# A two-branch graph convolution on one core: part of the row sums of tiles 4 to 11 taken from blocks that are loaded anyway

## The reference

```
d    = (sum(adj, axis=1) + 1e-9) ** -0.5
H_f  = relu((d[:,None] * adj * d[None,:] @ x)         @ W_f + b_f)
H_s  = relu((d[:,None] * adj * d[None,:] @ spatial_x) @ W_s + b_s)
attn = sigmoid(concat(H_f, H_s) @ W_att + b_att)
y    = x + attn * H_f + (1 - attn) * H_s
out  = (y - mean(y)) / sqrt(var(y) + 1e-5)          # over a row
```

## Time and profile before

| | |
|---|---|
| median of 3 runs | 420.37 us (420.26 to 420.81) |
| the profiled execution | 420.79 us, of which 419.0 us are its span |
| mean granted clock of PE | 0.971 |
| PE matmuls | 375.0 us busy, 90%, x1680 |
| PE weight loads | 309.4 us busy, 74% |
| DVE | 289.3 us busy, 69% |
| ACT | 286.1 us busy, 68% |
| POOL | 146.3 us busy, 35% |
| DMA | 132.84 MB, mean 317 GB/s |

### The profile page before, as it was taken

The page is one execution under the profiler, slowest core; times in us unless marked ns, Lnnn a source line. Parts: engine busy times, 40 slices in busy tenths (PEclk is TensorE's granted clock), DMA queues, the critical chain, the costliest instruction groups (busy, mean ns, idle before and its releaser), DMA issues. The chain is left out here.

```text
span 419.0 us, 5128 instructions
## 1 busy us (share of the span) xinstructions
PE 375.0 (90%) x1680; PEld 309.4 (74%) x1680; DVE 289.3 (69%) x401; ACT 286.1 (68%) x346; POOL 146.3 (35%) x199
## 2 busy tenths in 40 slices
PE   0689998699969999999899999999999999998940
PEld 0567887588858887888678888888888888887830
DVE  2569983496366957597655959388757886977554
ACT  3768588877888749787888687674433676576453
POOL 1203001021000881059200899251000556643664
PEclk9999999999989999999989999999999999999965
DMA  8999999999999999999999999897555444350001
GB/s 312 389 425 421 417 422 421 421 421 420 422 420 422 415 342 418 422 419 422 423 418 422 413 415 375 320 380 268 199 190 187 192 128 165 111 175 27 25 26 51
DMA packets 25530, 132.84 MB, mean 317 GB/s; under 512 B 2848, under 2 KB 7712, under 8 KB 11296
## 3 DMA queue, kind: packets, MB, share of 16 engines
q1 hardware_dynamic: 25504, 132.53, 79.1%
HBM read 130.42 MB, written 2.10 MB: 316 GB/s over the span
## 5 line engine op out<-in xcount | busy, mean ns | idle before, releaser
L356 PE MATMUL sums<-Ah,Yh 128*128 128x512 f32 x512 | 203.4, 397 | 25.5 <-DVE Yl L432 18.3
L421 DVE TENSOR_TENSOR Al<-raw,Ah 128x2048 fp32r<-128x2048 f32 (+1 forms) x70 | 152.3, 2179 | 90.7 <-ACT Ah L552 89.5
L358 PE MATMUL sums<-Al,Yh 128*128 128x512 f32 x512 | 201.4, 393 | 0.0
L357 PE MATMUL sums<-Ah,Yl 128*128 128x512 f32 x512 | 201.3, 393 | 0.0
L552 ACT ACTIVATE Ah<-raw 128x2048 fp32r<-128x2048 f32 (+1 forms) x70 | 123.4, 1767 | 54.2 <-DMA raw<-in_At 30.2
L356 PEld LDWEIGHTS sums<-Ah,Yh 128*128 128x128 f32 x512 | 97.6, 191 | 49.0 <-DVE Yl L432 19.5
L565 ACT ACTIVATE nat<-nat 128x2048 f32<-128x2048 f32 x53 | 101.6, 1917 | 19.2 <-DMA nat<-in_adj 17.9
L358 PEld LDWEIGHTS sums<-Al,Yh 128*128 128x128 f32 x512 | 97.3, 190 | 20.7
L357 PEld LDWEIGHTS sums<-Ah,Yl 128*128 128x128 f32 x512 | 97.7, 191 | 19.8
L444 DVE TENSOR_TENSOR acc<-sums,acc 128x512 f32<-128x512 f32 x112 | 71.5, 682 | 6.3 <-PE sums L358 6.3
L657 POOL TENSOR_SCALAR dg<-rs 128x1 f32<-128x1 f32 x22 | 14.1, 640 | 150.6 <-ACT nat L565 150.3
(11 more groups left out here) (43 smaller groups left out, 112.1 us busy)
## 6 DMA issues: line engine op xcount, KB each, us to landing
raw<-in_At SPq DMA_DIRECT2D x63, 1024.0 KB, 10.0
nat<-in_adj SPq DMA_DIRECT2D x56, 1024.0 KB, 11.6
xs<-in_xs SPq DMA_DIRECT2D x7, 512.0 KB, 11.2
out<-xs SPq DMA_DIRECT2D x32, 64.0 KB, 1.7
raw<-in_At SPq DMA_DIRECT2D x4, 256.0 KB, 9.8
xs<-in_xs SPq DMA_DIRECT2D x1, 384.0 KB, 9.2
xs<-in_xs SPq DMA_DIRECT2D x1, 128.0 KB, 2.4
watt<-in_W_att SPq DMA_DIRECT2D x1, 128.0 KB, 10.3
```

What stands on the lines that cost most here:

```text
L356: pe.matmul(to, Yh[:, t % YRING, hs], high, start=first, stop=False)
L357: pe.matmul(to, Yl[:, t % YRING, hs], high, start=False, stop=False)
L358: mm = pe.matmul(to, Yh[:, t % YRING, hs], low, start=False, stop=last)
L421: dve.tensor_tensor(Al[:, k % SPLITS, a * IB:b * IB], raw[:, k % RAWS, a * IB:b * IB], Ah[:, k % SPLITS, a * IB:b * IB], ALU.subtract).the ...
```

## The change

1. Groups 1 and 2 (tiles 4 to 11) get the treatment of groups 6 and 7 in small. Their blocks of inner tiles below their own first tile (tiles 0 to 3 for group 1, 0 to 7 for group 2), 12 in items 0, 1, 4, 5 and 8 to 11, are added up by POOL in the planes of `S`; the first block of a plane is copied instead of added, and the clearing of `S` goes. PE sums the planes over partitions after items 6 and 12 (`collect_early`), DVE copies the sums to `early` ahead of the low parts of items 8 and 14 (`early_sums`), and POOL takes them as the third term of the degree. The parts of these tiles shrink to half of the remaining columns: 1792 for tiles 4 to 7, 1536 for tiles 8 to 11 (before, 2048).
2. The load of part 4 moves ahead of item 3; part 5 stays ahead of item 4.
3. Features: groups 1 to 7 are loaded after items 6, 12, 20, 28, 36, 39 and 43 (before: 6, 7, 15, 23, 31, 39, 47). `y_position` keeps the items of the Y of tiles 12 to 31.
4. The evacuation of the run that ends in items 15, 23 and 31 is done ahead of the low parts of items 17, 25 and 33.

```diff
+    EARLY_SUMS = {1: 6, 2: 12}
+    PLANE = {1: 0, 2: 1, G - 2: 0, G - 1: 1}
     parts = {k: [] for k in range(K)}
-    for k, r in [(0, 0), (1, 1), (4, 2), (5, 3), (8, 4), (9, 5), (10, 6), (11, 7)]:
+    for k, r in [(0, 0), (1, 1), (5, 3), (8, 4), (9, 5), (10, 6), (11, 7)]:
         parts[k] = [2 * r, 2 * r + 1]
+    parts[3], parts[4] = [4], [5]
...
-                if OWN_COLUMNS <= k < FINAL and runs[e][0] in BY_COLUMN]
+                if (OWN_COLUMNS <= k < FINAL and runs[e][0] in BY_COLUMN)
+                or (runs[e][0] in EARLY_SUMS and t < runs[e][0] * GT)]
 
     def blocks_summed(k):
         return sum(len(summed_blocks(i)) for i in range(k + 1))
 
+    def first_of_plane(k, j):
+        g = runs[items[k][j][0]][0]
+        return (k, j) == next((i, b) for i in range(K) for b in summed_blocks(i) if runs[items[i][b][0]][0] == g)
+    def last_summed(g):
+        return max(i for i in range(FINAL) for b in summed_blocks(i) if runs[items[i][b][0]][0] == g)
+    def own_columns(n):
+        g = tile_of(n) // GT
+        width = (N - g * IB) // 2
+        return g * IB + n % 2 * width, g * IB + (n % 2 + 1) * width
     SHARED = [0, 1, 3]
+    X_AFTER = {6: 1, 12: 2, 20: 3, 28: 4, 36: 5, 39: 6, 43: 7}
+    EVACUATE_FIRST = [k for k in range(K) if k < 2 * G or k in (17, 25, 33)]
...
@@ y_position
         free = (s - 1) * G + 2
+        if s in EARLY_SUMS:
+            return max(whole, free, EARLY_SUMS[s] + 2)
         return max(whole, free) if r < FULL else max(whole, free, COLLECT + 4)
...
@@ SP, load_part and the loop over items
+                if r // GT in EARLY_SUMS:
+                    a, b = own_columns(n)
+                    sp.dma_start(nat[:, n % NATS, 0:b - a],
+                                 adj[r * P:(r + 1) * P, a:b]).then_inc(nat_in[n % NATS], 16)
+                elif r < FULL:
                     sp.dma_start(nat[:, n % NATS, :], adj_v[r, n % 2]).then_inc(nat_in[n % NATS], 16)
...
                 load_item(k)
-                if k == 6:
-                    load_x(1)
-                if k % G == G - 1 and k // G + 2 < G:
-                    load_x(k // G + 2)
+                if k in X_AFTER:
+                    load_x(X_AFTER[k])
...
@@ PE
+            def collect_early(g, k):
+                pe.wait_ge(block_sum_ok, blocks_summed(last_summed(g)))
+                pe.wait_ge(evac_ok, 2 * (max(evac_no[e] for e in range(len(runs))
+                                             if runs[e][2] == 3 and end_item[e] <= k) + 1))
+                for q in range(GT):
+                    mm = pe.matmul(sums[:, 3, 0, q:q + 1], S[:, PLANE[g], q * P:(q + 1) * P], ones[:, :],
+                                   start=True, stop=True)
+                mm.then_inc(early_collected, 1)
...
+                        taken = [g for g in EARLY_SUMS if EARLY_SUMS[g] < k]
+                        if runs[e][2] == 3 and taken:
+                            pe.wait_ge(early_ok, taken[-1])
...
+                for g in EARLY_SUMS:
+                    if k == EARLY_SUMS[g]:
+                        collect_early(g, k)
...
@@ DVE
+            def early_sums(g):
+                dve.wait_ge(early_collected, g)
+                dve.tensor_tensor(early[:, g * GT:(g + 1) * GT], sums[:, 3, 0, 0:GT], tiny[:, :],
+                                  ALU.add).then_inc(early_ok, 1)
...
             for k in range(K):
                 ended = [e for e in evac_order if end_item[e] == k - 2]
-                evacuate_new(ended if k < 2 * G else ended[:1] if len(ended) == GT else [])
+                evacuate_new(ended if k in EVACUATE_FIRST else ended[:1] if len(ended) == GT else [])
                 if k == 1:
                     own_share(3)
+                for g in EARLY_SUMS:
+                    if k == EARLY_SUMS[g] + 2:
+                        early_sums(g)
...
@@ ACT, row_sum
-                    act.activation(nat[:, n % NATS, :], nat[:, n % NATS, :], ACT.Copy,
+                    a, b = own_columns(n) if r // GT in EARLY_SUMS else (0, N // 2)
+                    act.activation(nat[:, n % NATS, 0:b - a], nat[:, n % NATS, 0:b - a], ACT.Copy,
                                    accum_out=rs[:, r, h:h + 1]).then_inc(rs_act, 1)
...
@@ POOL, degree and sum_block
+                if r // GT in EARLY_SUMS:
+                    pool.wait_ge(early_ok, r // GT)
                 part_summed(pool, last_part(r))
-                pool.tensor_scalar(dg[:, r:r + 1], rs[:, r, 0:1], rs[:, r, 1:2], 1e-9,
+                third = early[:, r:r + 1] if r // GT in EARLY_SUMS else 1e-9
+                pool.tensor_scalar(dg[:, r:r + 1], rs[:, r, 0:1], rs[:, r, 1:2], third,
                                    ALU.add, ALU.add).then_inc(dg_ok, 1)
...
-                g = runs[items[k][j][0]][0] - BY_COLUMN[0]
+                g = runs[items[k][j][0]][0]
                 n = blocks_summed(k - 1) + summed_blocks(k).index(j)
                 raw_here(pool, k, j)
-                if n >= 1:
+                if first_of_plane(k, j):
+                    if g in BY_COLUMN:
+                        pool.wait_ge(early_collected, PLANE[g] + 1)
+                    pool.tensor_copy(S[:, PLANE[g], :], raw[:, k % RAWS, j * IB:(j + 1) * IB]).then_inc(block_sum_ok, 1)
+                else:
                     pool.wait_ge(block_sum_ok, n)
-                pool.tensor_tensor(S[:, g, :], S[:, g, :], raw[:, k % RAWS, j * IB:(j + 1) * IB],
-                                   ALU.add).then_inc(block_sum_ok, 1)
+                    pool.tensor_tensor(S[:, PLANE[g], :], S[:, PLANE[g], :], raw[:, k % RAWS, j * IB:(j + 1) * IB],
+                                       ALU.add).then_inc(block_sum_ok, 1)
...
-            pool.memset(S[:, :, :], 0.0).then_inc(pool_const, 1)
...
-            shared_degree(0)
-            shared_degree(1)
+            pool.wait_ge(pool_const, 6)
+            for r in range(PIECED):
+                shared_degree(r)
+                for j in summed_blocks(r):
+                    sum_block(r, j)
```

More of the change, by code:

```diff
@@ L221, in build @@
         dsum = sb("dsum", [P, T - FULL])
+        early = sb("early", [P, 3 * GT])
         share = sb("share", [P, GT])
@@ L240, in build @@
         column_ok = sem("column_ok")
+        early_collected = sem("early_collected")
+        early_ok = sem("early_ok")
         dg_ok = sem("dg_ok")
@@ L312, in load_part @@
                     part_summed(sp, n - NATS)
-                if r < FULL:
+                if r // GT in EARLY_SUMS:
[3 more added lines that the diff above has]
+                elif r < FULL:
                     sp.dma_start(nat[:, n % NATS, :], adj_v[r, n % 2]).then_inc(nat_in[n % NATS], 16)
@@ L489, in own_share @@
                                   ALU.add).then_inc(rs_dve, 1)
+            dve.wait_ge(pool_const, 6)
             own_share(0)
@@ L733, in _ @@
             pool.memset(share[:, :], -1.0 / F).then_inc(pool_const, 1)
-            pool.wait_ge(pool_const, 7)
-            shared_degree(0)
-            shared_degree(1)
+            pool.wait_ge(pool_const, 6)
[3 more added lines that the diff above has]
+                    sum_block(r, j)
             for k in range(2, FINAL):
```

## The result

The changed kernel takes **429.55 us** (428.33 to 430.14, 4 runs), the kernel before 420.44 us in the same comparison: ratio 1.0212, 95% interval 1.0193 to 1.0232. It is slower by 9.1 us, where 419.4 us was forecast and 417.2 to 421.6 us given as range. Its profiled execution took 430.14 us, its span is 428.3 us.

What follows compares the result with a forecast made beforehand. DMA was taken to limit up to item 40. Item 35 starting 3.1 us sooner less 2.2 us of half clock gains 0.9 us: 420.79 to 419.9 us profiled, median 0.42 us lower, 419.4 us; range 417.2 to 421.6 us.

Steps and rivals of the forecast that it cites:

- What bounds the kernel: DMA limits up to item 40; the end of the run is PE's start of item 35 plus a constant.
- The evacuations: Gaps in items 16 and 32 go, 9.2 us with restarts, lying wholly in PE's new gap ahead of item 35.
- The features of group 5: Landing at 214.0 us, they stall ACT 11.5 us at Yh of tile 20; PE starts item 35 at 221.0 us.
- half clock: PE restarts at half clock after the gap ahead of item 35, losing 1.5 to 2.9 us, taken as 2.2.
- the rival in which nothing waits: Group 5's features don't gate at tile 20: gain 5.8 to 7.4 us, some 414.0 us; chance 0.10.
- The bytes: Smaller parts of groups 1 and 2 save 3.0 loads, 7.46 us of DMA, all before item 19.
- item 12 on PE at about 86 us: A stated sign that the forecast holds: PE at item 12 at about 86 us.
- the saving doesn't reach item 36: Rival at items 8 to 10: tile 4's late Yh idles DMA; 2.5 us give 421.0 us; chance 0.16.
- The early waits: Ahead of items 9 to 11 Yl waits shrink, PE pays two column sums of 0.9 us: net 2.5 us.
- The early gaps: PE's three Yl waits ahead of items 9 to 11, 4.5 us, shrink to about 0.7 us.
- POOL's added sums and their contention with DVE: 12 operations; low parts of items 0, 1, 4, 5, 8 to 11 up to 1.9 us late, swallowed ahead of item 35.

Runs made afterwards that it cites:

- y4_x5_late: y4 with the features of group 5 loaded behind item 36 again, Yh of tile 20 still at item 34: 420.60 us.
- y4: Changed kernel with group 5's features behind item 31, tile 8's Y at item 16, sums of parts 10 and 11 ahead of tile 4's Yh: 413.55 us.
- x5_early: Changed kernel with the features of group 5 loaded behind item 31 as before, instead of behind item 36: 422.67 us.
- y4_no_evac: y4 without the three evacuations ahead of the low parts of items 17, 25 and 33: 414.01 us.

## Why the prediction was wrong

- **What bounds the kernel: right in the main.** DMA up to item 38, then POOL's block sums and degree, ACT's wait for it (3.60 us) and PE; the prediction had DMA up to item 40. The evacuations were priced as slack, and alone they moved the time by 0.2 us.
- **The features of group 5: right** in place and mechanism, and in the waits: ACT's 11.7 us for 11.5, PE's 8.8 us (where the rest was as described) for 9, half clock 2.4 to 2.5 us for 2.2. The cost was forecast too small: 5.4 us (419.4 less the 414.0 us of the rival in which nothing waits), measured 6.9, 7.0 and 7.3 us in three pairs of kernels. In y4_x5_late, 1.2 us above the forecast, 0.7 us of it is PE's later start of item 35 and 0.3 us the clock.
- **The bytes: this step failed.** "7.46 us of DMA less, all before item 19" is true of the bytes; that they would be worth it at item 36 needed DMA to stay full from item 3 to 36, and the prediction followed the queues for it, not every engine in order. 10.7 us of idle DMA, behind two waits of ACT (5.49 us at tile 4, 7.40 us at tile 8), took the place of 7.46 us gained. PE's item 35 came 10.1 us later than forecast, the end of the run 10.1 us. The first of the stated signs to fail was "item 12 on PE at about 86 us": it was 92.05 us, and 86.00 us in y4, where both waits are repaired.
- The rival "the saving doesn't reach item 36" had the right mechanism and, for half of it, the right place, with a chance of 0.16 and 2.5 us for its size. Its size was wrong mainly by one term: the degree of tile 4 was taken at 0.4 us and took 2.44 (Yh at 62.05 instead of 59.6 us; the other 0.4 us are PE's end of item 6, 57.67 instead of 57.2), and from there each us of wait was a us of idle DMA, because the issue of part 13 had no margin, as the text itself said. 4.5 us of idle DMA, and 5.2 us by its repair.
- The other half, tile 8 at item 14, was missed altogether. The early waits were costed from PE's side ("PE pays two column sums", 0.9 us each, and so they were: 0.8 us to the next matmul), not from the side of those who wait for the sums. The kernel before already shows how far ahead ACT is: it made the high part of item 14 from 91.6 us on, while PE was in item 12 until 95.0 us. An order of ACT for item 14 that waits for the end of item 12 on PE is a wait by construction. 6.2 us idle, 3.9 us by its repair alone; the rest is in part the spread of x5_early's runs and stays open.
- The early gaps were to shrink to 0.7 us; they were 1.37 and 2.56 us ahead of items 9 and 11, the second with half clock behind it, for the same reason: in y4 both are gone.
- POOL's added sums and their contention with DVE: right that they delay a low part by about 1 us (3.34 us for item 5) and that this ends in slack, wrong in leaving out the smallest of POOL's instructions, the degree, which is on the path.
- Two slips in the sums change nothing: the terms shown for the evacuations add up to 8.9 us (5.5 and 2 x 1.7), not 9.2, and those of the forecast to 419.5 us, not 419.4.

By repairs, made in this order, the 16.0 us from 429.55 to 413.55 are 6.9 (group 5's features), 3.9 (tile 8) and 5.2 us (tile 4), the first two each to about 1 us.

## What to carry to other kernels

A load that is saved is only saved if every engine behind the queue keeps its pace: follow each added wait on the engine that works furthest ahead, not only on the one that does the added work, and ask which buffers stand behind it. When a schedule says at which step a result is made, compare it with the step at which the consumer reaches it, for each engine's own lead. A wait that cannot be removed can be filled: two 1.7-us sums moved ahead of it were worth 5.2 us here.

## What the runs showed of the hardware

A one-column degree on POOL took 2.44 and 2.45 us when it started within 0.1 us of a 2.29-us two-input instruction of DVE, and 0.37 to 0.38 us beside none (the other three of the eight, beside the end of one, 0.87 to 1.03 us); the 22 of the kernel before took 0.30 us in the median and 2.31 at most. "SBUF — State Buffer", section "Who interferes with whom" of the Trainium skill, has the one engine wait out the other; the trace agrees, and it is the short instruction that pays the full length of the long one. PE came back from gaps of 9.69 and 8.80 us at half clock (the lower level, 1.2 GHz; granted 0.50 from 231.2 to 235.9 us behind the first) for 4.8 and 5.2 us, and from one of 2.73 us (y4_no_evac) for 3.7 us.
